# Cross attention with a ternary feed-forward: output product in PSUM banks of its own, and projection and value products split into halves of the rows that swap tiles

## The chip, the cores and the metric

One NeuronCore of a Trainium2 chip runs the whole program. The metric is device time in microseconds (us) of one execution. An engine is written as the profile writes it: PE is TensorE's matmuls, PEld its weight loads, DVE VectorE, ACT ScalarE, POOL GpSimd, SP the engine that issues most DMAs.

## What is computed

64 batches of 512 rows and 512 features go through a cross attention on 77 context rows and then through a feed-forward product with ternary weights. Cut to what matters:

```python
qh = einsum('bse,ehd->bshd', layernorm(x), Wq)   # 16 heads of 32, 4 groups of 4
kh = einsum('bse,ehd->bshd', ctx, Wk)            # 4 heads
vh = einsum('bse,ehd->bshd', ctx, Wv)
scores = einsum('bghsd,bhad->bhsa', rope(qh), rope(kh))   # sums over the groups g
attn = softmax(scores / 32 ** 0.5)
out = einsum('bhsa,bhad->bhsd', attn, vh).mean(axis=1)    # mean over the heads
x = x + out @ Wo
n = layernorm(x)
i_scale = max(abs(n)) / 127                      # one number for all of x
x = x + (round(n / i_scale) @ ternary(weight).T) * w_scale * i_scale + bias
```

Since the scores sum over the groups, the kernel adds the four groups of Wq first, and projects to 128 columns in place of 512. The quantisation scale needs the maximum over all of x, so the feed-forward product begins only when the attention of all batches is done.

## The kernel before

Three stages follow one another. In the first, 39 tiles of context rows become keys and values, which go to DRAM. In the second, the attention, the unit of work is a pair of tiles of 128 rows; 64 batches are 128 pairs (`NP_`). In the third, the feed-forward product, the unit is a batch. The change touches the second stage, and a few lines that prepare its constants in the first.

In the attention each engine has its own `step(i, k, g)`, and `steps` calls it for i = 0 to 134. A step works on up to eight pairs at once, each in another phase: `PROJ, ROPE, SCORE, VALUE, HEAD, RESID, STAT, RSTD` are lags 0 to 7, so that step i projects pair i, computes scores of pair i-2, values of pair i-3, adds the output product of pair i-5. From step 5 to step 127 all phases that PE serves are there. The order within a step is written out by hand for each engine, engines run their own instructions in that order, and semaphores are all that ties them.

- **PE** (L1139 to L1237): `halves` (L1131, its transposes are at L1136) turns 128 rows with two transposes of 64 rows each, which write to two PSUM banks. A step transposes the rotated queries `qr_sb`, the outputs `ost_sb`, the input `x_sb` and the exponentials `e_sb`; then come the scores (L1199, halves of the rows, fp32), the projection (L1210, 8 matmuls of 128 rows and 128 columns, fp32, `q_done`), the output product (L1221, 2 matmuls of 128 rows and 512 columns, fp32r, `y_done_t`) and the values (L1233, 6 matmuls of 103 rows and 136 columns, fp32, `pv_done`). An fp32 matmul of the source is two passes in the trace, an fp32r matmul and a transpose are one.
- **ACT** (L653 to L731) copies what PE leaves in PSUM to SBUF: `pv_sb` (L672), `qT_sb` (L683), `oT_sb` (L691), `xT_sb` twice (L700), `pT_sb` twice (L712), a square of x1 with its sum (L663), `q_sb` (L722, waits for `q_done`), the two exponentials (L729), the second square.
- **DVE** (L884 to L950): reciprocal, variance, absolute maximum (L903), first `bn_stats` (L910), two maxima and two subtractions on the scores (L918, L922), second `bn_stats` (L930), the two additions of the output product to x (L940, `added_t`), `bn_aggr` (L947), `ve_sb` (L949).
- **POOL** (L536 to L596): the rotation of q, the sum over heads, and the output split into a high and a rest part, `ost_sb` (L579, L585), which with `wst` (the same split of Wo, at DVE L817 to L821) makes fp32r products good for fp32.

PSUM has eight banks, in four tiles of two: `xT_ps` holds the transposed input, and then the output product (`bank[0]`, `bank[1]`); `qo_ps` the transposed queries and outputs, and the projection (`bank[2]`); `sc_ps` the scores; `pT_ps` the transposed exponentials and then the value product (`bank[6]`). Since input and output product share `xT_ps`, PE's transposes of x wait for `added_t` of the pair before:

```python
                    if isinstance(j, int) and j <= RESID:
                        at_least(pe, xT_copied_t, 2 * j)
                    else:
                        held(added_t, 2 * (j - RESID), added_count, 2)
```

Of the kernel before, what the change touches and what calls it, by code (L numbers as in the profile page):

```python
# [31 lines left out]
B, S, E = 64, 512, 512  # L32
CTX = 77
HEADS, GROUPS, D = 4, 4, 32
HD = HEADS * D
# [15 lines left out]
STARTS = [c * CR if (c + 1) * CR <= SC else SC - CR for c in range(CHUNKS)]  # L51
# [13 lines left out]
ZEROED = 7  # L65
# [23 lines left out]
def segments():  # L89

    out = []
    for c, start in enumerate(STARTS):
        for h in range(HEADS):
            lo, hi = max(c * CR, CTX * h), min(start + CR, CTX * (h + 1))
            if lo < hi:
                out.append((c, lo - start, hi - lo, h, lo - CTX * h))
    return out


def build(nc, x, ctx_in, wq, wk, wv, wo, fw, fb, ident_d, qcos_d, qsin_d, kcos_d, ksin_d, out):  # L100
# [11 lines left out]
    with stack:  # L112
# [57 lines left out]
        wst = sb("wst", [P, E], F32R)  # L170
# [10 lines left out]
        def early(*shape):  # L181
# [24 lines left out]
        woc = early(E)  # L206
# [17 lines left out]
        xT_ps, qo_ps, sc_ps, pT_ps = (  # L224
            stack.enter_context(nc.psum_tensor(n, [P, 2, 512], F32)) for n in ("xT_ps", "qo_ps", "sc_ps", "pT_ps"))
        bank = [ps[:, n, :] for ps in (xT_ps, qo_ps, sc_ps, pT_ps) for n in range(2)]
# [5 lines left out]
        def scores_of(t):  # L232
# [39 lines left out]
        rinv_ready, o_part, o_ready, ost_ready, wq_mean, wq_centred = (  # L272
            sem(n) for n in ("rinv_ready", "o_part", "o_ready", "ost_ready", "wq_mean", "wq_centred"))
        wq_summed = sem("wq_summed")
        oT_done, oT_copied, y_done_t, added_t, sq_done, amax_done = (
            sem(n) for n in ("oT_done", "oT_copied", "y_done_t", "added_t", "sq_done", "amax_done"))
# [63 lines left out]
        def _(sp):  # L340
            for n in range(CRING):
# [156 lines left out]
        def _(pool):  # L498
# [36 lines left out]
            def step(i, k, g):  # L535
                proj, rope, score, value, head, resid, stat, rstd = (stage(i, k, g, lag) for lag in range(RSTD + 1))  # L536
                if rope:
# [11 lines left out]

                    at_least(pool, qT_done, j - 1)  # L550
# [4 lines left out]
                if head:  # L555
# [7 lines left out]
                    pool.wait_ge(o_part, 2 * j + 1)  # L563
                    pool.tensor_tensor(pw2_sb[:, :, :, :], pw_sb[:, :, 0:2, :], pw_sb[:, :, 2:4, :],
                                       ALU.add).then_inc(o_part, 1)
                if rope:

                    j, kj, gj = rope
                    pool.wait_ge(stats_ready, j + 1)
                    pool.tensor_tensor(rs_sb[:, kj, :], ve_sb[:, kj % 4, :], mhalf[:, :], ALU.pow)\  # L570
                        .then_inc(rs_ready, 1)
                if head:
                    j, kj, gj = head
                    pool.wait_ge(o_part, 2 * j + 2)
                    pool.tensor_tensor(o_sb[:, :, :], pw2_sb[:, :, 0, :], pw2_sb[:, :, 1, :],
                                       ALU.add).then_inc(o_ready, 1)

                    at_least(pool, oT_done, j)
                    pool.tensor_tensor(ost_sb[:, :, :, 0, :],  # L579
                                       pw2_sb[:, :, 0, 0:D].unsqueeze(2).broadcast_to([P, 2, 2, D]),  # L580
                                       pw2_sb[:, :, 1, 0:D].unsqueeze(2).broadcast_to([P, 2, 2, D]),
                                       ALU.add).then_inc(o_ready, 1)

# [192 lines left out]
        def _(dve):  # L776
# [107 lines left out]
            def step(i, k, g):  # L884
# [58 lines left out]
                if proj:  # L943

                    j, kj, gj = proj
                    for t in range(2):
                        dve.bn_aggr(mv_sb[:, kj, t, :], bn_sb[:, t, :]).then_inc(mv_ready, 1)  # L947
# [378 lines left out]
```

## Time and profile before

| | before |
|---|---|
| median of 3 runs | 1268.47 us (1267.71 to 1268.85) |
| the profiled execution | 1268.9 us |
| its span, first to last instruction | 1267.0 us |
| PE busy | 1201.2 us, 95% of the span |
| DVE busy | 1124.7 us, 89% |
| ACT busy | 1001.1 us, 79% |
| POOL busy | 794.2 us, 63% |
| mean granted TensorE clock | 0.991 |

Busy is the time in which at least one instruction of the engine was under way. A row of a group of instructions gives its line, engine, operation, tiles out<-in, shape, count, then busy us and the mean ns of one. In the timeline a row is a run of like instructions: start us, us from the first start to the last end, engine, line, what, count.

### The profile page before, as it was taken

How to read it: one execution, taken by the hardware profiler on the slowest of the kernel's cores; microseconds unless marked ns; L12 is line 12 of the kernel's file. 1: busy time of each engine (PE TensorE's matmuls, PEld its weight loads, DVE VectorE, ACT ScalarE, POOL GpSimd, SP SyncE). 2: the span in 40 equal slices, each digit the busy share in tenths (PEclk: the TensorE clock that was granted, in tenths of full speed). 3: DMA queues.
4: the chain of work that ended last, by engine and by line, in shares of the span. 5: the costliest groups of instructions: out<-in, count | busy, mean ns of one | idle time of the engine just before them, and what ended most of it. 6: DMA issues, size and time to landing. Idle time of an engine off the chain costs nothing.

```text
span 1267.0 us, 42077 instructions
## 1 busy us (share of the span) xinstructions
PE 1201.2 (95%) x12408; PEld 983.0 (78%) x12471; DVE 1124.7 (89%) x2410; ACT 1001.1 (79%) x2339; POOL 794.2 (63%) x1536
## 2 busy tenths in 40 slices
PE   7999999999999999999999999999789999999997
PEld 7998888888888888888888888888645555555554
DVE  4656999999999999999999999999878888888887
ACT  4566888888888888888888888888768888888886
POOL 4767898898998988989989889899700000000000
PEclk9999999999999999999999999999889999999999
DMA  9772555555555555555555543323029999999945
GB/s 291 225 205 66 160 178 169 173 173 170 164 178 166 178 168 175 170 174 162 182 163 181 164 123 94 87 84 84 2 99 398 403 396 398 399 408 396 395 206 212
DMA packets 97241, 260.26 MB, mean 205 GB/s; under 512 B 42538, under 2 KB 53994, under 8 KB 76723
## 3 DMA queue, kind: packets, MB, share of 16 engines
q1 hardware_dynamic: 97154, 259.75, 59.6%
q8 instruction: 16, 0.26, 0.1%
q14 instruction: 23, 0.18, 0.0%
q10 hardware_dynamic: 48, 0.07, 0.0%
HBM read 137.11 MB, written 122.64 MB: 205 GB/s over the span
## 4 chain that ended last, share of the span: by engine, by line
DVE 44%; PE 35%; issue 15%; DVEq 3%; ACT 1%; POOL 1%; DMA 0%; SPq 0%; POOLq 0%; ACTq 0%
DVE amax L903 10%; PE pT_ps L1265 10%; PE sc_ps L1265 9%; DVE x_sb L940 8%; DVE mx_sb L918 7%; DVE bn_sb L930 6%; DVE e_sb L922 6%; PE qo_ps L1069 5%; PE xT_ps L1256 5%; DVE bn_sb L910 3%; PE sc_ps L1263 2%; DVE mv_sb L947 2%; DVE rinv_sb L890 2%; PE xT_ps L1058 1%; PE pT_ps L1263 1%
## 5 line engine op out<-in xcount | busy, mean ns | idle before, releaser
L1210 PE MATMUL qo_ps<-wqs,xT_sb 128*128 128x128 f32 x2048 | 262.6, 281 | 0.9 <-ACT xT_sb L700 0.9
L1210 PEld LDWEIGHTS qo_ps<-wqs,xT_sb 128*128 128x128 f32 x2048 | 238.2, 191 | 21.5 <-issue 20.0
L1233 PEld LDWEIGHTS pT_ps<-v_blk,pT_sb 103*128 103x128 f32 x1536 | 197.3, 190 | 11.8 <-ACT pT_sb L712 0.9
L940 DVE SCALAR_TENSOR_TENSOR x_sb<-x_sb,mv_sb,xT_ps 128x512 f32 (+1 forms) x256 | 180.0, 745 | 25.5 <-DVE bn_sb L930 10.8
L1233 PE MATMUL pT_ps<-v_blk,pT_sb 103*128 103x136 f32 x1536 | 200.1, 280 | 0.3 <-ACT pT_sb L712 0.3
L1008 DVE TENSOR_TENSOR x_sb<-x_sb 128x512 f32 (+1 forms) x256 | 164.7, 684 | 1.2 <-ACT x_sb L758 1.2
L700 ACT ACTIVATE xT_sb<-xT_ps 128x512 f32<-128x512 f32 x256 | 139.1, 595 | 33.3 <-PE xT_ps L1136 28.9
L663 ACT ACTIVATE sq_sb<-x_sb 128x512 bf16 (+1 forms) x256 | 162.4, 634 | 0.6 <-DVE x_sb L940 0.2
L903 DVE TENSOR_REDUCE amax<-x_sb (+1 forms) x128 | 154.6, 1208 | 0.3 <-issue 0.3
L758 ACT ACTIVATE x_sb<-pT_ps,mean,cols 128x512 f32<-128x512 f32 x128 | 99.5, 777 | 63.6 <-PE pT_ps L1265 63.6
L1265 PE MATMUL pT_ps<-wT,x_sb 128*128 128x512 f16 x512 | 131.4, 379 | 3.2
L1265 PE MATMUL sc_ps<-wT,x_sb 128*128 128x512 f16 x512 | 132.3, 381 | 0.2 <-issue 0.2
L1000 DVE TENSOR_SCALAR x_sb<-xT_ps 128x1024 f16<-128x1024 f16 x128 | 88.5, 692 | 44.3 <-PE xT_ps L1256 42.7
L729 ACT ACTIVATE e_sb<-e_sb,rs_sb 128x308 f32<-128x308 f32 x256 | 126.0, 542 | 1.4 <-DVE e_sb L922 1.4
L722 ACT ACTIVATE q_sb<-qo_ps 128x256 f32<-128x256 f32 x128 | 49.1, 384 | 98.1 <-PE qo_ps L1210 98.1
L1136 PE MATMUL xT_ps<-ident,x_sb 64*128 64x64 f32 x2048 | 91.1, 227 | 33.6 <-DVE x_sb L940 24.9
L918 DVE TENSOR_REDUCE mx_sb<-sc_ps 128x4 f32<-128x308 f32 x256 | 107.7, 460 | 10.6 <-PE sc_ps L1199 10.5
L1136 PEld LDWEIGHTS xT_ps<-ident,x_sb 64*128 64x128 f32 x2048 | 77.3, 138 | 46.9 <-issue 46.7
L712 ACT ACTIVATE pT_sb<-pT_ps 103x384 f32<-103x384 f32 x256 | 111.9, 499 | 1.0 <-PE pT_ps L1136 0.9
L922 DVE TENSOR_TENSOR e_sb<-sc_ps,mx_sb 128x308 f32<-128x308 f32 x256 | 108.7, 464 | 0.0
L559 POOL TENSOR_TENSOR pw_sb<-pv_sb,rinv_sb 128x264 f32<-128x264 f32 x128 | 80.5, 629 | 38.6 <-DVE rinv_sb L890 38.6
L545 POOL TENSOR_TENSOR qa_sb<-q_sb,qcos 128x256 f32<-128x256 f32 x128 | 93.4, 730 | 17.2 <-ACT q_sb L722 12.1
(135 smaller groups left out, 2673.7 us busy)
## 6 DMA issues: line engine op xcount, KB each, us to landing
out_y<-x_sb SPq DMA_DIRECT2D x112, 1024.0 KB, 6.5
x_sb<-in_x SPq DMA_DIRECT2D x128, 512.0 KB, 3.9
x_sb<-out_y SPq DMA_DIRECT2D x48, 1024.0 KB, 8.9
x_sb<-in_ctx SPq DMA_DIRECT2D x38, 256.0 KB, 4.0
k_blk<-k_scr SPq DMA_DIRECT2D x256, 9.6 KB, 1.7
v_scr<-x_sb SPq DMA_DIRECT2D x38, 68.0 KB, 3.0
k_scr<-x_sb SPq DMA_DIRECT2D x38, 64.0 KB, 3.3
v_blk<-v_scr SPq DMA_DIRECT2D x128, 10.2 KB
```

The costliest lines, as they stand in the source:

```text
L663: act.activation(sq_sb[:, :], x1_at(kj, gj, t), ACT.Square, accum_out=ssq[:, bass.ds(2 * j + t, 1)]).then_inc(sq_done, 1)
L700: act.activation(xT_sb[:, t, :, :].rearrange("p c (h r) -> p c h r", h=2), rows_of(xT_ps, t * E // 2, EC), ACT.Copy).then_inc(xT_copied_t, 1)
L729: act.activation(e_sb[:, kj % 2, t, :], e_sb[:, kj % 2, t, :], ACT.Exp, scale=rs_sb[:, kj, t:t + 1]).then_inc(exp_done_t, 1)
L903: dve.tensor_reduce(amax[:, bass.ds(2 * j, 2)], x1_at(kj, gj).rearrange("p (t e) -> p t e", t=2), AX.X, ALU.max, apply_absolute_value=True ...
L918: dve.tensor_reduce(mx_sb[:, t, :].rearrange("p (n h) -> p n h", n=2), scores_of(t), AX.X, ALU.max).then_inc(mx_ready, 1)
L922: dve.tensor_tensor(e_sb[:, kj % 2, t, :].rearrange("p (n h a) -> p n h a", n=2, a=CTX), scores_of(t), mx_sb[:, t, :].rearrange("p (n h) - ...
L940: dve.scalar_tensor_tensor(out=x1_at(kj, gj, t), in0=x_sb[:, kj // 2, 2 * (kj % 2) + t, :], scalar=mv_sb[:, kj, t, 0:1], in1=bank[t][:, :] ...
L1008: dve.tensor_tensor(x1_tile, x1_tile, u_sb[:, t, :], ALU.add).then_inc(sum_done_t, 1)
L1136: last = pe.transpose(ps[0:src.shape[1], n, at0:at0 + HALF], src[lo:hi, :], ident[lo:hi, lo:hi])
L1210: last = pe.matmul(bank[2][:, t * HD:(t + 1) * HD], xT_sb[:, t, c, :], wqs[:, c, :], start=c == 0, stop=c == EC - 1)
L1233: last = pe.matmul(bank[6][:, t * HEADS * VC:(t + 1) * HEADS * VC], pT_sb[0:CR, t, c * P:(c + 1) * P], v_blk[0:CR, slot, c, :, :].rearrang ...
L1265: last = pe.matmul(bank[4 + t][:, :], q16T_sb[:, t, c, :], wT[:, c, :], start=False, stop=c == EC - 1)
```

## The change

The tile `qo_ps` becomes `y_ps` and holds the output product alone. The transposed queries and outputs go to the columns of `sc_ps` behind the scores (308 on), the projection to `xT_ps` once the transposed input is copied out. So PE's first transposes of a step wait for the subtractions (`sub_done_t`) of the step before, the transposes of x for `q_copied` instead of `added_t`, the scores for `oT_copied` too, and the output product for the addition before it.

The output is no longer split in two parts: `o_sb` and `wst` are plain fp32, `ost_sb` and its two POOL instructions go, both tiles' outputs are transposed together, and the output product is two fp32 matmuls of 64 rows, tile 0 on rows 0 to 63 and tile 1 on rows 64 to 127, each to its bank. It stands right behind the scores, ahead of the projection.

Projection and values are split by rows. `project(0)` multiplies the upper 64 rows of tile 0 and, alternating with it, the lower 64 rows of tile 1; `project(1)` takes the halves left over, adding to the same banks, once `q_half` tells that the first are done. `values` does so too, with 64 rows and 68 columns (two heads) a matmul in place of 103 rows and 136 columns; the three chunks of `e_sb` are now 128 columns wide and overlap. The order is `project(0)`, `values(0)`, `project(1)`, `values(1)`. On DVE the scores come first in a step, maximum and `bn_aggr` later; on POOL the power for `rs_sb` comes a step later.

```diff
-STARTS = [c * CR if (c + 1) * CR <= SC else SC - CR for c in range(CHUNKS)]
+STARTS = [min(c * CR, SC - P) for c in range(CHUNKS)]
...
-        xT_ps, qo_ps, sc_ps, pT_ps = (
-            stack.enter_context(nc.psum_tensor(n, [P, 2, 512], F32)) for n in ("xT_ps", "qo_ps", "sc_ps", "pT_ps"))
+        xT_ps, y_ps, sc_ps, pT_ps = (
+            stack.enter_context(nc.psum_tensor(n, [P, 2, 512], F32)) for n in ("xT_ps", "y_ps", "sc_ps", "pT_ps"))
...
+            pool.memset(wst[:, :], 0.0).then_inc(zeroed, 1)
+            pool.memset(o_sb[:, :, :], 0.0).then_inc(zeroed, 1)
...
-                    pool.tensor_tensor(ost_sb[:, :, :, 0, :],
-                                       pw2_sb[:, :, 0, 0:D].unsqueeze(2).broadcast_to([P, 2, 2, D]),
-                                       pw2_sb[:, :, 1, 0:D].unsqueeze(2).broadcast_to([P, 2, 2, D]),
-                                       ALU.add).then_inc(o_ready, 1)
-
-                    pool.wait_ge(o_ready, 2 * j + 2)
-                    pool.tensor_tensor(ost_sb[:, :, :, 1, :],
...
-                    act.activation(oT_sb[:, :, :].rearrange("p c (h r) -> p c h r", h=2), rows_of(qo_ps, P, 2),
+                    act.activation(oT_sb[:, :].rearrange("p (c h r) -> p c h r", c=1, h=2), rows_of(sc_ps, SC + P, 1),
                                    ACT.Copy).then_inc(oT_copied, 1)
...
-                    act.activation(q_sb[:, :], bank[2][:, 0:2 * HD], ACT.Copy).then_inc(q_copied, 1)
+                    act.activation(q_sb[:, :].rearrange("p (t n) -> p t n", t=2), xT_ps[:, :, 0:HD], ACT.Copy)\
+                       .then_inc(q_copied, 1)
...
                 if score or resid:
 
-                    at_least(pe, q_copied, min(i, NP_) if isinstance(i, int) else i)
+                    at_least(pe, sub_done_t, 2 * (min(i - SCORE, NP_) if isinstance(i, int) else i - SCORE))
...
-                    pe.wait_ge(x_in[kj], gj * 16 + 16)
-
-                    if isinstance(j, int) and j <= RESID:
-                        at_least(pe, xT_copied_t, 2 * j)
-                    else:
-                        held(added_t, 2 * (j - RESID), added_count, 2)
+                    if not isinstance(j, int) or j > 0:
+                        held(q_copied, j, q_count, 1)
...
+                if resid:
+
+                    j, kj, gj = resid
+                    at_least(pe, added_t, 2 * j)
+                    pe.wait_ge(oT_copied, j + 1)
+                    for t in range(2):
+                        rows = slice(t * HALF, (t + 1) * HALF)
+                        last = pe.matmul(y_ps[:, t, :], oT_sb[rows, :], wst[rows, :], start=True, stop=True)
+                    last.then_inc(y_done, 1)
+                def project(second):
+
+                    for c in range(EC):
+                        for n in range(2):
+                            rows, t = slice(n * HALF, (n + 1) * HALF), n ^ second
+                            last = pe.matmul(xT_ps[:, t, 0:HD], xT_sb[rows, t, c, :], wqs[rows, c, :],
+                                             start=second == 0 and c == 0, stop=second == 1 and c == EC - 1)
+                            if second == 0 and c == EC - 1:
+                                last.then_inc(q_half, 1)
+                    return last
+
+                def values(second, slot):
+
+                    for c in (0, 2, 1):
+
+
+                        for n in range(2):
+                            rows, t = slice(n * HALF, (n + 1) * HALF), n ^ second
+                            last = pe.matmul(pT_ps[:, t, c * VC:(c + 2) * VC], pT_sb[rows, t, c * P:(c + 1) * P],
+                                             v_blk[rows, slot, c, c:c + 2, :].rearrange("p h d -> p (h d)"),
+                                             start=second == 0 and c == 0, stop=second == 1 and c == 1)
+                            if second == 0 and c == 1:
+                                last.then_inc(pv_half, 1)
+                    return last
...
+                    pe.wait_ge(xT_copied_t, 2 * proj[0] + 2)
+                    project(0)
...
+                    values(0, slot)
+                if proj:
+                    pe.wait_ge(q_half, 2 * proj[0] + 2)
+                    project(1).then_inc(q_done, 1)
+                if value:
+                    pe.wait_ge(pv_half, 2 * value[0] + 2)
+                    values(1, slot).then_inc(pv_done, 1)
```

On PE, from the scores of a step to the first transposes of the next, this stood before (`qT_sb` are the transposed queries, `xT_sb` the transposed input, `oT_sb` the transposed outputs, `pT_sb` the transposed exponentials, `qr_sb` the rotated queries; in brackets the semaphores waited for):

```order
L1199 MATMUL sc_ps<-k_blk,qT_sb 128x154 [waits qT_copied,sub_done_t,k_in0]
L1199 MATMUL sc_ps<-k_blk,qT_sb 128x154 x3
L1210 MATMUL qo_ps<-wqs,xT_sb 128x128 [waits xT_copied_t,oT_copied]
L1210 MATMUL qo_ps<-wqs,xT_sb 128x128 x3
L1210 MATMUL qo_ps<-wqs,xT_sb 128x128 [waits xT_copied_t]
L1210 MATMUL qo_ps<-wqs,xT_sb 128x128 x3
L1221 MATMUL xT_ps<-wst,oT_sb 128x512 [waits oT_copied]
L1221 MATMUL xT_ps<-wst,oT_sb 128x512
L1233 MATMUL pT_ps<-v_blk,pT_sb 128x136 [waits pT_copied_t]
L1233 MATMUL pT_ps<-v_blk,pT_sb 128x136 x5
L1136 MATMUL qo_ps<-ident,qr_sb 128x64 [waits qr_ready,q_copied]
L1136 MATMUL qo_ps<-ident,qr_sb 128x64 x3
```

The same stretch in the changed kernel, from the scores to the end of the step:

```order
L1199 MATMUL sc_ps<-k_blk,qT_sb 128x154 [waits qT_copied,oT_copied,k_in0]
L1199 MATMUL sc_ps<-k_blk,qT_sb 128x154 x3
L1209 MATMUL y_ps<-wst,oT_sb 128x512 [waits oT_copied,added_t]
L1209 MATMUL y_ps<-wst,oT_sb 128x512
L1216 MATMUL xT_ps<-wqs,xT_sb 128x128 [waits xT_copied_t]
L1216 MATMUL xT_ps<-wqs,xT_sb 128x128 x7
L1229 MATMUL pT_ps<-v_blk,pT_sb 128x68 [waits pT_copied_t]
L1229 MATMUL pT_ps<-v_blk,pT_sb 128x68 x5
L1216 MATMUL xT_ps<-wqs,xT_sb 128x128 [waits q_half]
L1216 MATMUL xT_ps<-wqs,xT_sb 128x128 x7
L1229 MATMUL pT_ps<-v_blk,pT_sb 128x68 [waits pv_half]
L1229 MATMUL pT_ps<-v_blk,pT_sb 128x68 x5
```

The output product has moved ahead of the projection, and a part of the values stands between the projection's two parts, whose last matmul signals `q_done`.

The changed kernel's step begins on PE like this (`o_sb` are the outputs, no longer split):

```order
L1141 MATMUL sc_ps<-ident,qr_sb 128x64 [waits qr_ready,sub_done_t,x_in6]
L1141 MATMUL sc_ps<-ident,qr_sb 128x64 x3
L1141 MATMUL sc_ps<-ident,o_sb 128x64 [waits o_ready]
L1141 MATMUL sc_ps<-ident,o_sb 128x64
L1141 MATMUL xT_ps<-ident,x_sb 128x64 [waits q_copied]
L1141 MATMUL xT_ps<-ident,x_sb 128x64 x15
L1141 MATMUL pT_ps<-ident,e_sb 128x64 [waits exp_done_t,pv_copied]
L1141 MATMUL pT_ps<-ident,e_sb 128x64 x11
```

The transposes of x, which waited for `added_t` before, now wait for `q_copied`, those of the outputs for `o_ready`, and the first of all for `sub_done_t`.

ACT's order is that of before, with other line numbers; from one `q_sb` copy to the `oT_sb` copy of the next step it reads, in the changed kernel:

```order
L719 ACTIVATE q_sb<-xT_ps 128x256 [waits rope_mul]
L726 REGISTER_ALU [waits rs_ready]
L727 ACTIVATE e_sb<-e_sb,rs_sb 128x308 [waits sub_done_t]
L726 REGISTER_ALU
L727 ACTIVATE e_sb<-e_sb,rs_sb 128x308 [waits sub_done_t]
L660 ISA [waits sq_done,added_t]
L660 ACTIVATE sq_sb,ssq<-x_sb 128x512
L669 ACTIVATE pv_sb<-pT_ps 128x272 [waits o_part,pv_done]
L680 ACTIVATE qT_sb<-sc_ps 128x256 [waits sc_done,oT_done,qT_done]
L688 ACTIVATE oT_sb<-sc_ps 128x128 [waits y_done,oT_done]
```

Nothing moved here: the copy of q, two exponentials, a square, and the copies of the value product, the queries and the outputs stand in the same order in both kernels.

## Rows read from the trace of the kernel before

**Rows 1.** The page's first lines: span, busy us and share of each engine.
```profile
span 1267.0 us, 42077 instructions
...
PE 1201.2 (95%) x12408; PEld 983.0 (78%) x12471; DVE 1124.7 (89%) x2410; ACT 1001.1 (79%) x2339; POOL 794.2 (63%) x1536
```

**Rows 2.** 400 to 600 us: length, PE, PEld, DVE, ACT, POOL busy (x count), granted clock, DMA.
```profile
400.00:600.00 200.00, 191.02 (x2334) 175.56 (x2333) 191.78 (x443) 167.26 (x442) 180.72 (x346) 1.00 0.54 171
```

**Rows 3.** The first `bn_stats` of a step (L910): min/median/max ns, first and last start.
```profile
L910 DVE BATCH_NORM_STATS2 bn_sb<-x_sb x128: 646/678/686, 91.6 to 892.4; 128x6 f32<-128x512 f32 x128
```

**Rows 4.** Timeline of one step and the next one's scores, PE.
```profile
453.26 0.72 PE L1136 MATMUL xT_ps<-ident,x_sb 64*128 64x64 f32 x16 [0.15 <-issue]
...
453.78 0.74 PE L1136 MATMUL pT_ps<-ident,e_sb 64*103 64x64 f32 x12
...
454.33 0.78 PE L1199 MATMUL sc_ps<-k_blk,qT_sb 64*128 64x154 f32 x8
...
455.04 2.05 PE L1210 MATMUL qo_ps<-wqs,xT_sb 128*128 128x128 f32 x16
...
456.84 0.72 PE L1221 MATMUL xT_ps<-wst,oT_sb 128*128 128x512 f32 x2
...
457.40 1.55 PE L1233 MATMUL pT_ps<-v_blk,pT_sb 103*128 103x136 f32 x12
...
460.65 0.77 PE L1199 MATMUL sc_ps<-k_blk,qT_sb 64*128 64x154 f32 x8
```

**Rows 5.** The same timeline, ACT.
```profile
454.02 1.09 ACT L700 ACTIVATE xT_sb<-xT_ps 128x512 f32<-128x512 f32 x2 [0.16 <-PE xT_ps L1136]
...
454.99 0.87 ACT L712 ACTIVATE pT_sb<-pT_ps 103x384 f32<-103x384 f32 x2
...
457.20 0.38 ACT L722 ACTIVATE q_sb<-qo_ps 128x256 f32<-128x256 f32 x1 [0.73 <-PE qo_ps L1210]
...
457.49 0.98 ACT L729 ACTIVATE e_sb<-e_sb,rs_sb 128x308 f32<-128x308 f32 x2
...
458.37 0.62 ACT L663 ACTIVATE sq_sb<-x_sb 128x512 bf16 x1
...
458.99 0.40 ACT L672 ACTIVATE pv_sb<-pT_ps 128x272 f32<-128x272 f32 x1
...
459.44 0.39 ACT L683 ACTIVATE qT_sb<-qo_ps 128x256 f32<-128x256 f32 x1
...
459.71 0.38 ACT L691 ACTIVATE oT_sb<-qo_ps 128x256 fp32r<-128x256 f32 x1
```

**Rows 6.** The same timeline, DVE.
```profile
455.48 0.84 DVE L918 TENSOR_REDUCE mx_sb<-sc_ps 128x4 f32<-128x308 f32 x2
...
457.01 0.68 DVE L930 BATCH_NORM_STATS2 bn_sb<-x_sb 128x6 f32<-128x512 f32 x1
...
457.94 1.41 DVE L940 SCALAR_TENSOR_TENSOR x_sb<-x_sb,mv_sb,xT_ps 128x512 f32 x2 [0.24 <-DVE bn_sb L930]
...
461.70 0.84 DVE L918 TENSOR_REDUCE mx_sb<-sc_ps 128x4 f32<-128x308 f32 x2
```

**Rows 7.** Instructions by line and shape: x count, busy us, mean ns.
```profile
L1210 PEld LDWEIGHTS qo_ps<-wqs,xT_sb 128*128 128x128 f32 x2048 | 238.2, 191 | 21.5 <-issue 20.0 <-ACT xT_sb L700 1.5
...
L1136 PEld LDWEIGHTS xT_ps<-ident,x_sb 64*128 64x128 f32 x2048 | 77.3, 138 | 46.9 <-issue 46.7
L1199 PEld LDWEIGHTS sc_ps<-k_blk,qT_sb 64*128 64x128 f32 x1024 | 76.0, 187 | 0.2 <-issue 0.2
...
L585 POOL TENSOR_TENSOR ost_sb<-o_sb,ost_sb 128x128 fp32r<-128x128 f32 x128 | 57.9, 453 | 10.0
...
L637 ACT ACTIVATE x_sb<-sc_ps 128x128 f32<-128x128 f32 x38 | 10.5, 277 | 3.6 <-PE sc_ps L1077 0.2
...
L1069 PEld LDWEIGHTS qo_ps<-wkv_parts,cT_parts 128*64 128x64 f32 x12 | 1.4, 134 | 0.0
...
L502 POOL MEMSET v_blk<- 128x816 f32 x1 | 0.8, 782 | 0.0
```

More of the change, by code:

```diff
@@ L548, in step @@
                                            ALU.mult).then_inc(rope_mul, 1)
+                if score:
+                    j, kj, gj = score
+                    pool.wait_ge(stats_ready, j + 1)
+                    pool.tensor_tensor(rs_sb[:, kj, :], ve_sb[:, kj % 4, :], mhalf[:, :], ALU.pow)\
+                        .then_inc(rs_ready, 1)
+                if rope:
+                    j, kj, gj = rope
                     at_least(pool, qT_done, j - 1)
@@ L926, in step @@
                                           ALU.subtract).then_inc(sub_done_t, 1)
+                if rope:
+                    dve.wait_ge(bn_step, 2 * rope[0] + 2)
+                if rstd:
+                    j, kj, gj = rstd
+                    at_least(dve, rs2_ready, j - 1)
+                    dve.wait_ge(sq_done, 2 * j + 2)
+                    dve.tensor_scalar(ve2_sb[:, kj % 2, :], ssq[:, bass.ds(2 * j, 2)], 1.0 / E, EPS, ALU.mult, ALU.add)\
+                       .then_inc(var_ready, 1)
+                if rope:
+                    j, kj, gj = rope
+                    for t in range(2):
+                        dve.bn_aggr(mv_sb[:, kj, t, :], bn_sb[:, t, :]).then_inc(mv_ready, 1)
                 if proj:
                     j, kj, gj = proj
-                    dve.bn_stats(bn_sb[:, 1, :], x_sb[:, kj // 2, 2 * (kj % 2) + 1, :]).then_inc(bn_step, 1)
-                    dve.wait_ge(bn_step, 2 * j + 2)
+                    dve.wait_ge(x_in[kj], gj * 16 + 16)
+                    at_least(dve, mv_ready, 2 * j)
+                    dve.bn_stats(bn_sb[:, 0, :], x_sb[:, kj // 2, 2 * (kj % 2), :]).then_inc(bn_step, 1)
                 if resid:
@@ L1148, in step @@
                     for t in range(2):
-                        last = halves(qo_ps, t * HALF, qr_sb[:, kj % 2, t * HD:(t + 1) * HD])
+                        last = halves(sc_ps, SC + t * HALF, qr_sb[:, kj % 2, t * HD:(t + 1) * HD])
                     last.then_inc(qT_done, 1)
@@ L1183, in step @@
                         for c, start in enumerate(STARTS):
-                            last = halves(pT_ps, (t * CHUNKS + c) * HALF, e_sb[:, kj % 2, t, start:start + CR])
+                            last = halves(pT_ps, (t * CHUNKS + c) * HALF, e_sb[:, kj % 2, t, start:start + P])
                     last.then_inc(pT_done, 1)
@@ L1201, in step @@
                     last.then_inc(sc_done, 1)
-                if proj:
-                    j, kj, gj = proj
-                    if resid:
-                        pe.wait_ge(oT_copied, resid[0] + 1)
-                    for t in range(2):
-                        pe.wait_ge(xT_copied_t, 2 * j + t + 1)
-                        for c in range(EC):
-                            last = pe.matmul(bank[2][:, t * HD:(t + 1) * HD], xT_sb[:, t, c, :], wqs[:, c, :],
-                                             start=c == 0, stop=c == EC - 1)
-                    last.then_inc(q_done, 1)
@@ L1213, in step @@
                 if resid:
                     j, kj, gj = resid
+                    at_least(pe, added_t, 2 * j)
                     pe.wait_ge(oT_copied, j + 1)
-                    if not proj:
-                        pe.wait_ge(xT_copied_t, NT)
-                        pe.wait_ge(added_t, 2 * j)
                     for t in range(2):
-                        pe.matmul(bank[t][:, :], oT_sb[:, t, :], wst[:, :], start=True, stop=True)\
-                          .then_inc(y_done_t, 1)
+                        rows = slice(t * HALF, (t + 1) * HALF)
+                        last = pe.matmul(y_ps[:, t, :], oT_sb[rows, :], wst[rows, :], start=True, stop=True)
```

146 lines of the change are left out of this document (62 added, 84 removed).

## The prediction

> **What bounds the kernel now.** I read the page first: DVE and PE share the lead, and their shares over the whole span mix three stages [rows 1]. So I asked for the busy time in a stretch of the attention alone: of 200 us PE is busy 191.0, DVE 191.8, ACT 167.3, POOL 180.7, at full clock [rows 2]. Next I need the length of a step. The first `bn_stats` starts at 91.6 us in pair 0 and at 892.4 in pair 127, so 127 steps take 800.8 us, 6.30 us each [rows 3]. DVE then works 0.959 x 6.30 = 6.04 us a step, and no order of its work can go below that. Last I read one step in the timeline, each engine by itself [rows 4 to 6]. DVE runs almost without a hole; it stops for 0.24 us ahead of the additions, for its own `bn_stats` [rows 6]. PE goes from one job straight to the next [rows 4]. ACT alone has a hole that counts: 0.73 us before it copies q, which waits for the projection [rows 5]. That row is where to look, since the change moves the end of the projection.
>
> **How long PE's jobs will be.** The program now uses halves of 64 rows throughout. Its scores already do: 8 passes in 0.78 us, whose last one takes about 0.29, so a pass each 0.070 us and a pair of passes (one in each half of the rows) each 0.14 [rows 4]. The full passes: 16 of the projection take 456.84 - 455.04 = 1.80 us, 0.112 each; the values with 136 columns, (1.55 - 0.28) / 11 = 0.116 [rows 4]. Per column that is 0.87, 0.85 and (scores, 154 columns) 0.9 ns. So two halves together cost what one full pass costs, and this sets the prices:
>
> - *Projection*: 8 full matmuls of 2 passes become 16 pairs of passes of 128 columns, 0.112 us each. 1.79 us, as before, in two parts of 0.89.
> - *Output product*: 2 passes of fp32r, 457.40 - 456.84 = 0.56 us until the values begin, become 4 passes of fp32, two pairs of 512 columns. By 0.85 ns a column a pair takes 0.435, both 0.87 us. The lower bound takes the slope between 128 and 136 columns instead (4 ns for 8 columns): 0.112 + 384 x 0.0005 = 0.30, both 0.61. I take 0.87, since the scores' 154 columns lie on that line and not on the flatter one.
> - *Values*: 12 pairs of passes of 68 columns. Streaming alone would be 0.06, and the transposes of x (64 columns, the same 128 columns of weights) do run at (0.72 - 0.22) / 15 x 2 = 0.066 a pair. But their weight load takes 138 ns, and the load for an fp32 matmul takes 187 to 191 [rows 7]. A load of 64 columns takes 134, so 64 columns more cost 57 ns, and a load of 128 columns keeps its half busy for some 0.11 us. I take 0.112 a pair, set by loads: 1.34 us for both parts, as before, 0.67 each. The lower bound is 0.066, or 0.40 each.
> - *Transposes*: those of the outputs are halved, those of `e_sb` now have 128 columns of weights, and should go from (0.74 - 0.25) / 11 = 0.045 to the 0.033 of x. 12 of them save 0.15 us of PE, off the path below.
>
> PE's work in a step falls from about 6.0 to 5.7 us (also two changes between full and half rows are gone).
>
> **The path through ACT.** ACT is in order, and its order isn't changed: copy of q, two exponentials, square, copy of the value product, copy of the queries, copy of the outputs. The next step's scores need the last of these, and the next projection stands behind the scores on PE. This is a ring: end of projection, ACT, scores, projection. Before:
>
> - end of the projection to ACT's copy of q: 455.04 + 2.05 = 457.09, start 457.20: 0.11
> - copy of q to the end of the copy of the outputs: 457.20 to 460.09: 2.89 [rows 5]
> - handing over to PE, between 0.04 (last transpose 453.98, copy 454.02) and 0.11: 0.08
> - scores to projection 0.71, projection 2.05 [rows 4]
>
> 5.84 us, under 6.30: not binding. PE in fact began the scores only at 460.65, held by its own transposes. After:
>
> - the same 0.11 and 0.08
> - ACT 457.20 to 459.71, 2.51, and the copy of 128 instead of 256 columns, 0.28 [rows 7]: 2.79
> - scores until the output product begins: (0.78 - 0.29) + 0.14, 0.62
> - output product, now ahead of the projection: 0.87
> - `project(0)` 0.89, `values(0)` 0.67
> - `project(1)`: 7 pairs of 0.112 and the last pass with its end, 0.28: 1.07
>
> Sum 7.10 us. The ring is now longer than DVE's 6.04 and PE's 5.7, so it sets the step. In it the output product and half of the values have come ahead of the signal for the copy of q, and nothing that left it is as long. The copies of xT (1.09 us) and of pT (0.87) on ACT [rows 5] are ready: 2.0 us after the outputs' copy, while `values(0)` begins 2.46 after it. All steps from 5 to 127 have it, 123 of them. 123 x (7.10 - 6.30) = 98 us.
>
> **What costs nothing.** POOL loses two instructions, the second 0.45 us [rows 7]; it waits for q anyway. The power for `rs_sb` comes a step later, with more than 2 us in hand before the exponentials. The new wait of PE for `sub_done_t` holds the transposes of q and all behind them, but maxima and subtractions end some 1.7 us after the scores, and PE is busy with output product and projection for 3.5. The transposes of x wait for `q_copied`, 0.4 us after the projection, under `values(1)`. DVE's own stall of 0.24 us goes, and turns into waiting for scores. PE's wait for `added_t` before the output product is met over a step earlier. Two more memsets at the start are under 0.78 us together [rows 7], before matmuls that wait for loads. SP's queue keeps its order, and the feed-forward stage its code.
>
> Profiled execution: 1268.9 + 98 = 1367 us (span 1267.0, with 1.9 around it); the median shown is 1268.5, which is the same to 0.1%. I say **1367**.
>
> **Rivals.**
>
> *Loads and streams add up in a full pass.* A full pass would be 0.048 us of load and 0.5 ns a column, as the 128 and 136 columns allow; halves of alternating rows would hide more. Then the output product costs 0.61 and `values(0)` 6 x 0.082 = 0.49, the ring 6.66, and the time is 1268.9 + 123 x 0.36 = 1313. For it: the slope of those two rows. Against it: the scores at 0.14 a pair where this gives 0.125. Chance 0.17. The Trainium skill, "TensorE: Matmul & The Clock Gate", Part 3, says that a weight load overlaps with matmuls under way only when they are in another row group, which would be this case; the full fp32r passes of 512 columns here, 0.56 us for two with their loads, hardly leave room for it.
>
> *Faster: the halves run at the pace of the transposes.* If a pair of passes were limited by issue and not by columns, 0.066 for 128 and 68 columns alike, the projection would end after 0.53 + 0.40 + 0.74 and the output product take its lower bound of 0.61. The ring is 0.11 + 2.79 + 0.08 + 0.62 + 0.61 + 0.53 + 0.40 + 0.74 = 5.9. DVE binds at 6.04, and its stall of 0.24 is gone: 1268.9 - 123 x 0.26 = 1237. It decides once the PE part of the ring, 4.12 by my prices, falls by over 0.8. For it: DVE is the busiest engine, and 0.24 us of its stalls do go. Against it: the scores' pace with 154 columns. Chance 0.09.
>
> *The long halves do not overlap*, or the new hole on PE, about 1 us while it waits for ACT, lowers the granted clock, which was 1.00 throughout the attention. With four separate passes of 0.435 the ring grows to 7.97: 1268.9 + 123 x 1.67 = 1474. Against it: the scores do overlap, and PE still works 5.7 of 7.1 us. Chance 0.08.
>
> *No change within 0.2%* (2.5 us, about what a measurement of this kernel can tell): the ring would have to come out at 6.30 by chance. 0.03.
>
> **Numbers.** Forecast 0.63 and the first rival 0.17 make 0.80. Both lower bounds together give a ring of 6.57, so 1302; unpriced waits of 0.3 us a step, since each of eight handings over may cost 0.04 more, give 1404. Range 1302 to 1404. Slower by over 0.2%: 0.63 + 0.17 + 0.08 = 0.88; faster 0.09; the same 0.03.
>
> **What would show it.** Right: steps of about 7.1 us; ACT idle some 1.4 to 1.8 us a step before the copy of q, released by the projection; DVE idle some 1 us before the maxima, waiting for scores; two passes of the output product starting 0.43 apart from the next two; 12 pairs of value passes in 1.3 us. Wrong: DVE busy over 95% in the attention, or value pairs at 0.07, or scores that start well after the outputs' copy has ended, which would name another ring.

## The result, and the profile after

The changed kernel takes 1422.3 us (4 runs, 1419.4 to 1424.6) against 1268.3 for the one before: 1.121 times as long, 95% interval 1.119 to 1.123. Slower was forecast, and the ring through ACT is there; but the 1367 us and the range up to 1404 were too low. The step grew as said, and on top of it came a cause that the prediction had not asked about: PE's loop had become too long to be kept.

The page of the profiled execution (1419.35 us) shows span, busy time, the granted clock in 40 slices, and the queue that carries instructions (packets, MB, share of time):

```profile
span 1417.5 us, 48905 instructions
...
PE 1207.7 (85%) x15992; PEld 973.0 (69%) x16055; DVE 1103.7 (78%) x2409; ACT 960.0 (68%) x2339; POOL 696.5 (49%) x1282
...
PEclk9999999999999999999999999999987999999999
...
q8 instruction: 146, 2.39, 0.7%
```

Every engine is busy for a smaller share than in [rows 1]. The last line is new in size: 146 packets of instructions, where the kernel before has 16. The mean granted clock is 0.961 against 0.991.

The first `bn_stats` of a step (first and last start), and the busy times from 400 to 600 us:

```profile
L927 DVE BATCH_NORM_STATS2 bn_sb<-x_sb x128: 682/695/697, 92.1 to 1039.3; 128x6 f32<-128x512 f32 x128
```
```profile
400.00:600.00 200.00, 162.00 (x2706) 146.01 (x2703) 156.50 (x368) 130.58 (x368) 131.53 (x240) 0.95 0.46 144
```

(1039.3 - 92.1) / 127 = 7.46 us a step, against 6.30 [rows 3]. The forecast was 7.10. PE, DVE, ACT and POOL all have more holes than in [rows 2], and the clock is 0.95 in the midst of the attention.

But the timeline of a single ordinary step says less than 7.46. PE, ACT and DVE from 455 us on:

```profile
455.42 0.38 ACT L719 ACTIVATE q_sb<-xT_ps 128x256 f32<-128x256 f32 x1 [1.94 <-PE xT_ps L1216]
...
455.70 0.98 ACT L727 ACTIVATE e_sb<-e_sb,rs_sb 128x308 f32<-128x308 f32 x2
...
456.58 0.62 ACT L660 ACTIVATE sq_sb<-x_sb 128x512 bf16 x1
...
457.19 0.38 ACT L669 ACTIVATE pv_sb<-pT_ps 128x272 f32<-128x272 f32 x1
...
457.47 0.38 ACT L680 ACTIVATE qT_sb<-sc_ps 128x256 f32<-128x256 f32 x1
...
457.70 0.59 PE L1141 MATMUL pT_ps<-ident,e_sb 64*128 64x64 f32 x12 [1.06 <-ACT pv_sb L669]
457.74 0.28 ACT L688 ACTIVATE oT_sb<-sc_ps 128x128 f32<-128x128 f32 x1
...
457.89 1.10 ACT L697 ACTIVATE xT_sb<-xT_ps 128x512 f32<-128x512 f32 x2
...
458.12 0.79 PE L1199 MATMUL sc_ps<-k_blk,qT_sb 64*128 64x154 f32 x8
...
458.71 1.05 PE L1209 MATMUL y_ps<-wst,oT_sb 64*128 64x512 f32 x4
...
459.01 0.86 DVE L898 TENSOR_REDUCE mx_sb<-sc_ps 128x4 f32<-128x308 f32 x2 [1.00 <-PE sc_ps L1199]
...
459.57 1.09 PE L1216 MATMUL xT_ps<-wqs,xT_sb 64*128 64x128 f32 x16
...
460.46 0.82 PE L1229 MATMUL pT_ps<-v_blk,pT_sb 64*128 64x68 f32 x12
...
461.08 1.14 PE L1216 MATMUL xT_ps<-wqs,xT_sb 64*128 64x128 f32 x16
...
462.03 0.81 PE L1229 MATMUL pT_ps<-v_blk,pT_sb 64*128 64x68 f32 x12
...
462.34 0.38 ACT L719 ACTIVATE q_sb<-xT_ps 128x256 f32<-128x256 f32 x1 [1.98 <-PE xT_ps L1216]
```

From one copy of q (455.42) to the next (462.34) it is 6.92 us, and the ring of the prediction can be read row by row. ACT is held 1.98 us before the copy of q, by the projection, where it was 0.73 before [rows 5]; DVE is held 1.00 us before the maxima, by the scores; PE is held 1.06 us before it transposes `e_sb`, by ACT's copy of the value product.

The ordinary steps stand in groups of seven. Between them, at the turn of PE's loop, stands this (PE's timeline; then, for single microseconds, busy times of PE, PEld, DVE, ACT, POOL, and the clock):

```profile
435.45 0.79 PE L1229 MATMUL pT_ps<-v_blk,pT_sb 64*128 64x68 f32 x12
440.79 0.48 PE L1141 MATMUL sc_ps<-ident,qr_sb 64*128 64x64 f32 x4 [4.54 <-issue]
...
443.76 1.94 PE L1209 MATMUL y_ps<-wst,oT_sb 64*128 64x512 f32 x4
445.47 1.37 PE L1216 MATMUL xT_ps<-wqs,xT_sb 64*128 64x128 f32 x16
446.67 0.80 PE L1229 MATMUL pT_ps<-v_blk,pT_sb 64*128 64x68 f32 x12
...
448.23 0.80 PE L1229 MATMUL pT_ps<-v_blk,pT_sb 64*128 64x68 f32 x12
```
```profile
438.00:439.00 1.00, 0.00 (x0) 0.00 (x0) 0.64 (x2) 0.00 (x0) 0.98 (x2) 1.00 0.04 2
439.00:440.00 1.00, 0.00 (x0) 0.00 (x0) 0.00 (x0) 0.00 (x0) 1.00 (x2) 0.63 0.05 7
440.00:441.00 1.00, 0.21 (x4) 0.24 (x6) 0.00 (x0) 0.00 (x0) 0.00 (x0) 0.50 0.20 19
...
444.00:445.00 1.00, 1.00 (x5) 0.50 (x4) 0.96 (x3) 0.72 (x3) 0.00 (x0) 0.50 0.00 0
...
446.00:447.00 1.00, 1.00 (x22) 1.00 (x20) 1.00 (x2) 0.00 (x0) 1.00 (x2) 0.95 0.00 0
```

PE ended its values at 436.24 and does nothing for 4.54 us, with "issue" as the reason: no semaphore is missing. POOL, DVE and ACT run out of work behind it, until by 440 us all four are idle. In that hole the granted clock falls to half (1.2 GHz), and the output product then takes 1.94 us in place of 1.05, the first part of the projection 1.37 in place of 1.09. From values to values (435.45 to 448.23) this step takes 12.8 us, where an ordinary one takes 6.9. The waits of PE over the whole span:

```profile
PE pT_ps L1141 <- ACT pv_sb L669: 116.2, 111, 1.5
PE sc_ps L1141 <- issue: 31.5, 7, 4.6
PE sc_ps L1141 <- POOL qr_sb L563: 26.3, 7, 4.1
```

116.2 us behind ACT's copy of the value product is the ring's hole. 31.5 us for "issue" in 7 pieces and 26.3 for `qr_sb` in 7 are turns, 14 in all: the loop runs 15 times, so it jumps back 14 times. The second name misleads: the queries that PE transposes after a turn are made a step earlier, and the row named is the next pair's, which POOL worked on while PE stood still.

Two more readings of the trace, which no view above prints, name the jump itself. The record of PE's branch at the loop's end (one of the instructions that don't count as busy) takes 4.1 to 5.3 us at each of the 14 jumps back and 0.08 the fifteenth time, when the loop ends; in the kernel before it takes 0.21 to 0.23 at a jump. And from one such branch to the next the instruction queue moves 8 to 10 packets, nearly always 9, where in the kernel before it moves none.

### The profile page after: what moved, and what is told of

The parts are those of the page before. It is cut to its first block, busy times and chain, and to the rows that moved or that the text cites. A ratio compares the mean times of both kernels' runs of the same rounds, so it can differ in the third digit from the quotient of the medians.

```text
span 1417.5 us, 48905 instructions
## 1 busy us (share of the span) xinstructions
PE 1207.7 (85%) x15992; PEld 973.0 (69%) x16055; DVE 1103.7 (78%) x2409; ACT 960.0 (68%) x2339; POOL 696.5 (49%) x1282
## 4 chain that ended last, share of the span: by engine, by line
PE 76%; issue 10%; ACT 6%; POOL 4%; DVE 2%; ACTq 1%; POOLq 0%; DMA 0%; DVEq 0%; SPq 0%
PE xT_ps L1216 15%; PE pT_ps L1229 10%; PE pT_ps L1282 9%; PE sc_ps L1282 8%; PE y_ps L1209 8%; PE sc_ps L1199 6%; PE pT_ps L1141 5%; PE y_ps L1074 4%; PE xT_ps L1273 4%; ACT sq_sb L660 2%; ACT pv_sb L669 2%; PE sc_ps L1141 2%; PE sc_ps L1280 2%; PE xT_ps L1063 1%; PE pT_ps L1280 1%
## 5 line engine op out<-in xcount | busy, mean ns | idle before, releaser
L1216 PEld LDWEIGHTS xT_ps<-wqs,xT_sb 64*128 64x128 f32 x4096 | 270.7, 191 | 63.6 <-issue 35.3
L1216 PE MATMUL xT_ps<-wqs,xT_sb 64*128 64x128 f32 x4096 | 285.7, 278 | 2.8 <-ACT xT_sb L697 2.3
L578 POOL TENSOR_TENSOR rs<-ve_sb,mhalf 128x2 f32 (+1 forms) x128 | 89.7, 701 | 247.3 <-DVE ve_sb L915 247.3
L1229 PE MATMUL pT_ps<-v_blk,pT_sb 64*128 64x68 f32 x3072 | 206.8, 265 | 0.2
L1229 PEld LDWEIGHTS pT_ps<-v_blk,pT_sb 64*128 64x128 f32 x3072 | 198.0, 189 | 2.6 <-issue 1.2
L936 DVE SCALAR_TENSOR_TENSOR x_sb<-x_sb,mv_sb,y_ps 128x512 f32 (+1 forms) x256 | 177.9, 736 | 5.2 <-PE y_ps L1209 5.2
L1141 PE MATMUL pT_ps<-ident,e_sb 64*128 64x64 f32 x1536 | 79.4, 238 | 116.3 <-ACT pv_sb L669 116.2
L1141 PEld LDWEIGHTS pT_ps<-ident,e_sb 64*128 64x128 f32 x1536 | 65.6, 147 | 128.6 <-issue 124.1
L1209 PE MATMUL y_ps<-wst,oT_sb 64*128 64x512 f32 x512 | 145.2, 638 | 1.7 <-DVE x_sb L936 1.0
L709 ACT ACTIVATE pT_sb<-pT_ps 128x384 f32<-128x384 f32 x256 | 115.4, 525 | 0.4 <-PE pT_ps L1141 0.4
```

What stands on the lines that cost most here:

```text
L709: act.activation(pT_sb[:, t, :].rearrange("p (c h r) -> p c h r", c=CHUNKS, h=2), rows_of(pT_ps, t * CHUNKS * HALF, CHUNKS), ACT.Copy).the ...
L936: dve.scalar_tensor_tensor(out=x1_at(kj, gj, t), in0=x_sb[:, kj // 2, 2 * (kj % 2) + t, :], scalar=mv_sb[:, kj, t, 0:1], in1=y_ps[:, t, :] ...
L1141: last = pe.transpose(ps[0:src.shape[1], n, at0:at0 + HALF], src[lo:hi, :], ident[lo:hi, lo:hi])
L1209: last = pe.matmul(y_ps[:, t, :], oT_sb[rows, :], wst[rows, :], start=True, stop=True)
L1216: last = pe.matmul(xT_ps[:, t, 0:HD], xT_sb[rows, t, c, :], wqs[rows, c, :], start=second == 0 and c == 0, stop=second == 1 and c == EC - 1)
L1229: last = pe.matmul(pT_ps[:, t, c * VC:(c + 2) * VC], pT_sb[rows, t, c * P:(c + 1) * P], v_blk[rows, slot, c, c:c + 2, :].rearrange("p h d ...
```

## Experiments

Theory A from here on: two causes. A ring of 6.9 us a step, and a stall at each turn of PE's loop, because it now holds 1725 instructions in place of 1291 and is loaded again each time. (The counts are the instructions that the trace shows on PE from one branch to the next. The expectations below were written with counts that are off by 2 to 11, 1731 for 1725, 1631 for 1633, 1531 for 1538, about 1280 for 1291, and with 15 turns where there are 14 jumps back.)

### PE's steps written out, in both kernels

```diff
-            steps(pe, step)
+            for i in range(NP_ + RSTD):
+                step(i, i % UN, i // UN)
```

For the changed kernel:

> The changed kernel, with PE's attention steps written out one after the other, no loop on PE; all other engines keep theirs. Theory A (two causes: a ring of 6.9 us a step, and a stall at each of the 15 turns of PE's loop because its longer code must be loaded again): the 15 long steps of about 12.2 us fall to 6.9, saving 15 x 5.3 = 80 us, so about 1342 us, granted clock 0.99, and the other steps stay at 6.91 us. Rival (PE's clock falls by itself once PE is idle 1 us a step, and the long steps come from that): the drops to half clock stay, about 1400 to 1420 us.

Measured: 1346.7 us (ratio to before 1.062, interval 1.060 to 1.064). 75.6 us less than with the loop, 5.4 for each of the 14 jumps back. Not all of it need be the stall, since the kernel before, which has none, gains 4.8 by the same edit. Window and `bn_stats` starts:

```profile
400.00:600.00 200.00, 170.15 (x2958) 153.29 (x2958) 172.11 (x407) 143.02 (x407) 144.25 (x261) 1.00 0.49 157
```
```profile
L927 DVE BATCH_NORM_STATS2 bn_sb<-x_sb x128: 684/695/696, 90.3 to 964.5; 128x6 f32<-128x512 f32 x128
```

(964.5 - 90.3) / 127 = 6.88 us on average, so no long step is left but the one of 14 us at the start, which every kernel here has in some form. The clock is 1.00 although PE still has its hole of a microsecond in each step: those holes don't lower it, and the rival falls. What remains, 78 us, is the ring's; the two experiments on the ring below bear it out.

For the kernel before:

> The kernel before, with PE's attention steps written out in the same way. Every eighth step takes 7.16 instead of 6.23 us before. Theory A (that too is the turn of PE's loop): 15 x 0.93 = 14 us less, about 1255 us. Rival (the turn of another engine's loop, or the register waits): within 3 us of 1268.

Measured: 1263.8 us (0.996, 0.995 to 0.998). 4.8 us less instead of 14: the long step of 7.16 us (from copy of q to copy of q) stayed, so it wasn't PE's turn. Theory A was wrong here in its reading of the kernel before, and its PE loop cost at most 4.8 / 14 = 0.34 us at the turn.

### The long loop put into the kernel before

```diff
-            steps(pe, step)
+            for k in range(2 * UN):
+                step(k, k % UN, k // UN)
+            with pe.Fori(1, GRP // 2) as h:
+                for n in range(2):
+                    for k in range(UN):
+                        step((h * 2 + n) * UN + k, k, h * 2 + n)
+            for k in range(RSTD):
+                step(NP_ + k, k, GRP)
```

The registers that count in the loop start from values to match.

> The kernel before, with PE's loop of 8 steps made one of 16: the same instructions in the same order, but about 2560 in the loop instead of 1280, and 7 turns instead of 15. Theory A (a turn back over more code than is kept makes PE load it again): 7 turns of about 5 us each, at DVE's bound, 25 to 35 us more, near 1300 us, with steps of about 11 us at the turns and more packets on the instruction queue. Rival (the long steps belong to the changed kernel's work, not to the length of the loop): within 5 us of 1268.

Measured: 1307.3 us in one run, beside 1269.0 for the kernel before. 38.3 us; the loop runs 7 times and so jumps back 6 times, which makes 6.4 each. PE's timeline at one of them, and the instruction queue:

```profile
289.90 0.34 PE L1136 MATMUL qo_ps<-ident,qr_sb 64*128 64x64 f32 x4 [3.43 <-issue]
...
293.20 0.26 PE L1136 MATMUL pT_ps<-ident,e_sb 64*103 64x64 f32 x1 [1.50 <-issue]
...
294.85 3.67 PE L1210 MATMUL qo_ps<-wqs,xT_sb 128*128 128x128 f32 x16
...
302.33 2.05 PE L1210 MATMUL qo_ps<-wqs,xT_sb 128*128 128x128 f32 x16
```
```profile
q8 instruction: 98, 1.61, 0.5%
```

A stop of 3.43 us for "issue", one of 1.50 in the midst of the transposes of `e_sb`, and a projection of 3.67 us instead of 2.05 at half clock. The work, its order and every tile are those of the kernel before; only the length of the loop differs. So the stall belongs to the length, not to the halves of the rows. The branch's record takes 3.3 to 5.5 us at each of the 6 jumps, and from one to the next the instruction queue moves 12 packets, for 2578 instructions in the loop; in the changed kernel it was 9 for 1725.

### Fewer instructions in the changed kernel's loop

Values in full rows again, all of them behind the projection:

```diff
-                def values(second, slot):
+                def values(slot):
...
+                            last = pe.matmul(pT_ps[:, t, 0:HEADS * VC], pT_sb[:, t, c * P:(c + 1) * P],
+                                             v_blk[:, slot, c, :, :].rearrange("p h d -> p (h d)"),
+                                             start=c == 0, stop=c == CHUNKS - 1)
...
-                    values(0, slot)
```

> The changed kernel, with the value product in full rows again (6 matmuls of 128 rows and 136 columns in place of 12 of 64 rows and 68), all behind the projection. PE's loop falls from 1731 to about 1530 instructions. Theory A: values(0), 0.67 us, leaves the ring and a wait of some 0.2 between the projection's halves comes in, so steps of about 6.45 us; if 1530 instructions are kept without loading, the eighth step costs about 1 us more than the others, and the time is about 1300 us; if not, 5 us more, about 1360 us. Rival (code size has no part): the eighth step stays at 12 us.

Measured: 1319.5 us (one run).

```profile
q8 instruction: 18, 0.29, 0.1%
```
```profile
400.00:600.00 200.00, 194.89 (x2699) 166.45 (x2697) 176.45 (x420) 148.06 (x421) 148.38 (x271) 1.00 0.52 163
```
```profile
408.49 1.16 PE L1216 MATMUL xT_ps<-wqs,xT_sb 64*128 64x128 f32 x16 [0.18 <-PE xT_ps L1216]
409.58 1.66 PE L1226 MATMUL pT_ps<-v_blk,pT_sb 128*128 128x136 f32 x12
411.17 0.34 PE L1141 MATMUL sc_ps<-ident,qr_sb 64*128 64x64 f32 x4
```

18 packets, no long step at the turns, clock 1.00, and 0.2 us for the branch: with 1538 instructions the loop is kept. Steps are 6.67 us and not 6.45, since PE has become the bound, with 194.9 of 200 us: its 12 full passes take 411.17 - 409.58 = 1.59 us here, where the values by halves take about 1.3 in all, and it has a gap of 0.18 between the projection's halves, which `values(0)` used to fill.

The same in every second step only, the others by halves (`if kj % 2 == 0:` around both parts, and `pv_half` counted to match), which makes 1633 instructions:

> The changed kernel with PE's loop, and the value product in full rows in every second step only: 1631 instructions in the loop, between the 1531 that ran without a long step and the 1731 that had one of 12 us at each turn. If 1631 are kept: about 1340 us, steps between 6.7 and 6.9 us, and no packets beyond some 20 on the instruction queue. If not: 15 long steps, about 1415 us, and over 100 packets. Theory A says one or the other, and nothing between.

```profile
q8 instruction: 19, 0.31, 0.1%
```

1328.1 us (one run), 19 packets, steps of 6.64 to 6.73 and of 6.89 to 6.93 us by turns (medians of the starts of `bn_stats`) and none above: 1633 are kept, 1725 are not. That is 12 us under what I had said; with half of the steps 0.21 us shorter it should have been 1346.7 - 123 x 0.1 = 1334, so half of the miss is my sum's, and the rest is no more than the four runs with PE's steps written out differ among themselves (1342.1 to 1348.2).

### The ring, ACT's side

```diff
                 if stat:
                     square(0)
+                    square(1)
...
-                if stat:
-                    square(1)
```

> The changed kernel, with ACT's second square moved next to the first, ahead of the copy of q, into the hole of 1.9 us. Theory A (the ring through ACT sets the step): 0.62 us leave the ring, steps fall from 6.91 to about 6.3 us, 123 x 0.6 = 74 us less, about 1345 us, with the long step of each eighth kept. Rival (another path, through DVE or POOL, sets the step): under 10 us less.

Measured: 1360.9 us in one run, with the long steps kept (146 packets, clock 0.961). Ordinary steps on ACT:

```profile
409.34 0.38 ACT L720 ACTIVATE q_sb<-xT_ps 128x256 f32<-128x256 f32 x1 [1.03 <-PE xT_ps L1215]
409.62 0.98 ACT L728 ACTIVATE e_sb<-e_sb,rs_sb 128x308 f32<-128x308 f32 x2
410.51 0.38 ACT L669 ACTIVATE pv_sb<-pT_ps 128x272 f32<-128x272 f32 x1
...
415.66 0.38 ACT L720 ACTIVATE q_sb<-xT_ps 128x256 f32<-128x256 f32 x1 [1.06 <-PE xT_ps L1215]
```

415.66 - 409.34 = 6.32 us: the 0.61 us between the exponentials and the copy of the value product are gone from the step, and the time fell by 61 us. It was to be 74: 14 of the 123 steps hold a jump, where PE waits for its code and not for ACT, and gain nothing from the edit, and the branch's record takes 5.3 us on average there in place of 4.8. Both edits together:

> The changed kernel with both edits together: PE's steps written out, and ACT's second square next to the first. Theory A: the two causes add, steps of 6.28 us without long ones, 1347 - 123 x 0.61 = 1272 us. Rival (the stall at the turn and the ring overlap, so that one edit takes part of the other's gain): 1285 us or more.

Measured: 1273.4 us (one run). 1346.7 - 1273.4 = 73 us for the squares, 1360.9 - 1273.4 = 87 for the turns (76 without the squares): the causes add, within 12 us.

### The ring, PE's side

The output product moved from behind the scores to behind `project(1)`, with PE's steps written out:

```diff
-                if resid:
...
                     project(1).then_inc(q_done, 1)
+                if resid:
...
+                        last = pe.matmul(y_ps[:, t, :], oT_sb[rows, :], wst[rows, :], start=True, stop=True)
+                    last.then_inc(y_done, 1)
```

> The changed kernel with PE's steps written out, and the output product moved from behind the scores to behind project(1). Theory A (the ring): 0.86 us leave it, but project(0) now has to wait for the copies of the transposed input, 1.1 us after the scores begin instead of at once, so steps of about 6.5 us, and 1347 - 123 x 0.4 = 1298 us. Rival (the output product in fp32 has no part in the step's length): 1347 us; rival (the additions on DVE, now late, set the step): over 1310 us.

Measured: 1293.6 us (one run), 53 us less than with it in front; steps of 6.48 us. Of the 0.86 us that left the ring, PE's new wait for the copies of the input takes 0.34: the projection begins 0.93 us after the scores here (399.65 and 400.58) instead of 0.59. The remaining 0.1 us wasn't followed up.

Both halves of the projection together, ahead of both of the values (squares moved, PE's steps written out):

```diff
                     project(0)
+                    pe.wait_ge(q_half, 2 * proj[0] + 2)
+                    project(1).then_inc(q_done, 1)
...
                     values(0, slot)
-                if proj:
-                    pe.wait_ge(q_half, 2 * proj[0] + 2)
-                    project(1).then_inc(q_done, 1)
-                if value:
                     pe.wait_ge(pv_half, 2 * value[0] + 2)
                     values(1, slot).then_inc(pv_done, 1)
```

> As the last one, and both halves of the projection stand together, ahead of both halves of the values. Theory A: values(0), 0.62 us, leaves the ring, a wait of some 0.2 us for the projection's own first half comes in, so the ring is 5.85 us and DVE's 6.04 or PE's 5.9 bind: steps of about 6.15 us and 1255 us. Rival (PE's own order loses more at the waits for its halves than it gains): 1270 us or more.

Measured: 1277.4 us (1.007, 1.005 to 1.009), 4 us more than the one run without this edit (its own four runs are 1276.2 to 1280.1). It is the rival that held.

```profile
400.00:600.00 200.00, 194.67 (x3212) 169.87 (x3210) 184.18 (x440) 162.60 (x441) 155.66 (x283) 1.00 0.53 174
```
```profile
406.39 0.29 PE L1140 MATMUL sc_ps<-ident,qr_sb 64*128 64x64 f32 x4
...
409.00 2.31 PE L1215 MATMUL xT_ps<-wqs,xT_sb 64*128 64x128 f32 x32
411.15 1.54 PE L1228 MATMUL pT_ps<-v_blk,pT_sb 64*128 64x68 f32 x20
```

PE is the bound, 194.7 of 200 us. The projection takes 411.15 - 409.00 = 2.15 us in one piece, where its two parts take 0.89 and 0.95 when the values lie between. Within it, the first pass of the second half starts 0.34 us after the last of the first (409.82, 410.15), and in the values the same gap is 0.37 (411.66, 412.03), where neighbouring pairs are 0.11 apart. These are the waits for `q_half` and `pv_half`, and the alternation `project, values, project, values` was hiding both.

### A version that beats both

```diff
-            steps(dve, step)
+            for i in range(NP_ + RSTD):
+                step(i, i % UN, i // UN)
```

in the kernel before, with PE's steps written out too:

> The kernel before, with DVE's attention steps written out too, beside PE's. The 7.16 us of every eighth step stayed when PE alone was written out. Theory A (it is the turn of DVE's loop, the engine that binds): 15 x 0.93 = 14 us less than 1264, about 1250 us. Rival (the turn of ACT's or POOL's loop): 1264 us.

Measured: 1248.1 us (0.983, 0.982 to 0.985): 15.7 us less than with PE's alone, and the fastest kernel of the study.

```profile
400.00:600.00 200.00, 196.46 (x2413) 180.61 (x2413) 197.74 (x456) 171.94 (x456) 185.49 (x356) 1.00 0.57 177
```

DVE is at 197.7 of 200 us. By the starts of `bn_stats`, the eighth step goes from 7.04 us to 6.18, and all steps are 6.18 now, with the loops of ACT and POOL still there. So the eighth step was the turn of DVE's loop: 0.86 us at each of 14 jumps back on the engine that binds, 12 of the 15.7 us; the rest comes from the other steps. It isn't the branch alone, whose record takes 0.06 us there. In the kernel before, the absolute maximum (L903) starts 1.36 us after `ve_sb` (L949) at a turn (389.01, 390.37), and 0.31 in the step behind it (396.18, 396.49), where other steps have 0.3 to 0.65. Between the two stand the branch and several register instructions; which of them is the cost wasn't tried.

## Why the prediction was right and wrong

- **What bounds the kernel before**: right. DVE at 6.04 us of work a step; with its loop written out it comes to 6.18. I took the mean step of 6.30 as one kind, though, and it hid two: 6.23, and 7.16 in every eighth, from copy of q to copy of q. One look at the intervals between 128 starts would have shown a cost at each turn of a loop.
- **The ring through ACT**: right in mechanism and nearly in size. 6.92 us measured, 7.10 forecast. By its terms (forecast, measured): end of projection to copy of q 0.11, 0.12; ACT to the end of the outputs' copy 2.79, 2.60; handing over 0.08, 0.10; scores 0.62, 0.59; output product 0.87, 0.86; `project(0)` 0.89, 0.89; `values(0)` 0.67, 0.62; `project(1)` to its end 1.07, 1.14. The term that was off is ACT's: from the copy of the value product to that of the queries it is 0.28 us, not the 0.45 of [rows 5].
- **The sum**: 123 x (6.90 - 6.30) = 74 us by the measured step, 78 by the kernel with PE written out. The forecast was 98.
- **Prices of the halves**: right. Six pairs of value passes take 0.62, with 0.112 from pair to pair and 0.06 behind the first, and not the 0.066 of the transposes. That it is their loads that set this pace was the prediction's reason, and no run tests it. PE's work in a step came to 5.85 us (170.15 of 200, at 6.88 a step) and not to 5.7, which cost nothing, since PE doesn't bind. The rival of loads and streams that add up (0.61 for the output product, 0.49 for `values(0)`) is out, and so is that of the transposes' pace.
- **The step that failed**: the list of what costs nothing. It went through POOL, DVE, the memsets, SP's queue and the feed-forward stage, and doesn't name the jump back of PE's loop or the number of instructions in it, so the sum has that term at nothing without a reason. The 28 more passes a step, each with its load, took the loop from 1291 to 1725 instructions and across a limit between 1633 and 1725. The runs showed a stall of 4.1 to 5.3 us at each of 14 jumps, worth 75.6 us with all that goes with it, half of the 154 by which the kernel got slower.
- **The third rival** had the lower clock right and its cause wrong. Holes of a microsecond never lowered it; the holes of some 4.5 us at the turns did, and the stretches at half clock behind them are part of the 5.4 us a turn.

The Trainium skill, "Runtime: NRT & Kernel Launch", section "Instruction fetch mechanics", gives PE room for 2048 instructions, refilled in blocks of 256, and says that a taken branch to a place outside the current window of two pages makes the engine fetch that place first. That such a stall exists, the runs bear out. Where it sets in, they do not. By the two pages, 512 instructions, the loop of the kernel before would have stalled as well; with 1291 it didn't, nor did 1538 or 1633. By the 2048, 1725 would have been kept; here they were not. The measurement decides, and the limit of this case lies between 1633 and 1725. The packets of a turn are more than the loop needs: 1725 / 256 = 6.7 against 9, and 2578 / 256 = 10.1 against 12, so about two blocks more are loaded. Two blocks less than 2048 would leave 1536, and yet 1633 were kept; whether it matters how the loop lies on the blocks wasn't tried.

## What to carry to other kernels

Splitting a matmul doubles its instructions: before doing so inside a loop, count the instructions of one turn on that engine and look at the packets on the instruction queue, and if the loop gets too long, write it out. Work that is put ahead of a signal lengthens every ring that the signal is part of, even where the engine gets less to do: walk the ring through the in-order engines back to itself with start-to-start times, and put what nobody in it needs into the waiting engine's hole (the second square: 61 to 73 us). And look at the intervals of one instruction over all steps, not at their mean.

## What the hardware did that I had not expected

- A jump back over 1725 instructions of PE took 4.1 to 5.3 us, and together with the lower clock that followed cost up to 5.4 us a turn; over 1633 it took 0.2 us. The same steps written out, some 27,000 instructions in a row, had no stall.
- The chip granted full clock through holes of 1.06 us in every step, and half clock from within one of 4.54 us to some us behind it.
- The turn of DVE's loop, with 197 instructions in it, costs 0.86 us in the kernel before, and writing the loop out took 15.7 us off.
